# Block maxima and row sums of an attention kernel: partition reductions on GpSimd for f32 transpositions and products on TensorE

## The chip, the cores and the metric

The kernel runs on one core of one Trainium2 chip. A core has five engines with a queue of instructions each, which run in order within an engine and meet one another only through semaphores: TensorE (PE in the profile, its weight loads PEld), VectorE (DVE), ScalarE (ACT), GpSimd (POOL) and SyncE (SP), which here issues the DMAs. The metric is the time of one execution on the device in microseconds (us), the median of several runs.

## What is computed

One graph attention layer behind a layer norm, with 4096 rows of 512 numbers in float32 and a dense 4096x4096 mask:

```python
h = relu(layernorm(x))                        # 4096 x 512
q = h @ W_q.T + b_q;  k = h @ W_k.T + b_k;  v = h @ W_v.T + b_v
z = (q @ k.T) / sqrt(512) * adj               # 4096 x 4096
z = where(z == 0, -10000, z)
out = x + relu(softmax(z, axis=1) @ v)
```

The softmax of a row needs two numbers from all of its 4096 scores: their largest, and the sum of the exponentials.

## The kernel before

**Layout.** The 4096 queries are worked on in BLOCKS = 8 blocks `s` of QW = 512. Within a block the 4096 keys are taken in PAIRS = 16 pairs `j` of tiles with 128 keys each. Step `n = 16 s + j` is one pair of one block, 128 steps in all. Scores are held transposed: keys on the 128 partitions, the block's 512 queries along the row. A pair is a slot of 128 x 1024 f32 (two tiles), and `slots` is a ring of 20. So everything that a query needs from all keys has to be reduced in two stages: over pairs by DVE (`run_min`, `acc`), and over the 128 partitions.

**A step in the steady stretch.** PE forms the scores of pair `i = n + 19` in four pieces (`scores`, L503: seven products of 6 matmuls in f16 halves, as the score product is done with seven quarter products in place of eight), and between them adds step n's probabilities times v into four PSUM banks (`weigh_v`, L559, four calls of 6 matmuls, one for each 128 queries `t`). ACT copies each product out of PSUM (`copy_m1` L747, `copy_m2` L752, `copy_u2` L759, `copy_m7` L764, `copy_u4` L769, `copy_d` L774, `copy_c12` L781), forms the exponentials of step n+2 (`exp` L786) and their f16 upper half (`high_p` L793). DVE adds the products (`add_c11` L1085, `add_c2` L1093), multiplies by the mask (`weigh` L1101), turns zeros into the large value and flips the sign (`negate` L1105), keeps the running smallest (`see_min` L1114, L1117; in flipped sign the largest score is the smallest number), subtracts the floor (`lower` L1133), forms the lower f16 half (`low_p` L1140) and adds up the exponentials (`add_up` L1148, L1151).

**The end of a block's scores.** When j = 14 the scores of block s+1 are complete. DVE folds the two halves of `run_min` into `half_min` (`halve_min`, L1121, 128 x 512). PE transposes it in four pieces of 128 x 128 into a PSUM bank (`turn_min`, L571), DVE takes the smallest along each row (`columns_min`, L1126, into `col_min`), PE transposes each column, repeated 128 times, back (`widen_min`, L579), and ACT copies the bank to `floor_b` (`copy_floor`, L799). Each partition then holds the smallest value of each query, and `lower(16 (s+1))` can start. Behind it on ACT stand `exp` and `high_p` of the same pair, then `copy_c12` and the next pair's `copy_m1`.

**The row sums.** In the same step DVE folds `acc` into `row_acc` (`halve_acc`, L1157). In step j = 15 PE multiplies it, four pieces of 128 x 128, with a column of ones (`sum_rows`, L587), DVE takes the reciprocal out of PSUM (`row_gain`, L1163, L1165, into `row_out`), and ACT scales the four banks with it (`copy_o`, L808). `weigh_v` of the next block's first pair waits for `copy_o`, bank by bank.

**Order.** The order of each engine's instructions is written out by hand in the loops over n. The first block is different only in that its scores are formed while the projections still run; from step n = 109 on no scores are left, and PE runs `weigh_v` alone. GpSimd has almost nothing to do: memsets, the identity matrix `ident`, and two `partition_all_reduce` of 128 x 4 and 128 x 5 numbers for the scales of v and of the key-query product (L449). That operation leaves in every partition the reduction over all partitions, column by column.

Of the kernel before, what the change touches and what calls it, by code (L numbers as in the profile page):

```python
# [11 lines left out]
ABSMAX = bass.bass_isa.ReduceOp.absmax  # L12

P = 128
# [34 lines left out]
def adj_preln_attention(nc, x, adj_t, wq, bq, wk, bk, wv_t, bv, out, g_dram, v_dram, h_dram):  # L49
# [15 lines left out]
    with ctx:  # L65
# [6 lines left out]
        def sem(name):  # L72
            return ctx.enter_context(nc.semaphore(name))
# [20 lines left out]
        ones = sb("ones", [P, 1], F32)  # L94
        log_p = sb("log_p", [P, 1], F32)
        col_min = sb("col_min", [P, QT], F32)
# [80 lines left out]
        ones_ready = sem("ones_ready")  # L177
# [57 lines left out]
        min_turned = sem("min_turned")  # L235
        col_min_ready = sem("col_min_ready")
        min_wide = sem("min_wide")
# [7 lines left out]
        sums_ready = sem("sums_ready")  # L245
        inv_ready = sem("inv_ready")
# [191 lines left out]
        def _(pool):  # L438
            nc.gpsimd.memset(zeros[:, :], 0.0).then_inc(zeros_ready, 1)
            nc.gpsimd.memset(ident[:, :], 0.0).then_inc(ident_zero, 1)  # L440
            nc.gpsimd.memset(ones[:, :], 1.0).then_inc(ones_ready, 1)
            nc.gpsimd.memset(log_p[:, :], LOG_P_SCALE).then_inc(ones_ready, 1)
# [3 lines left out]
                                    ).then_inc(ident_ready, 1)  # L446
            for k in range(2):
                pool.wait_ge(mag_ready, k + 1)
                nc.gpsimd.partition_all_reduce(mag_all[k][:, :], mag[k][:, :], P, ABSMAX).then_inc(mag_reduced, 1)  # L449

        @block.tensor
        def _(pe):
# [55 lines left out]
            def scores(i, piece):  # L508
# [3 lines left out]
                if piece == 0:  # L512
# [10 lines left out]
                    if s >= 2 and j == 2:  # L523
                        pe.wait_ge(floor_ready, s)
                    if s >= 2 and j == 3:
                        pe.wait_ge(inv_ready, s - 1)
# [36 lines left out]

            def turn_min(s, bank):
                pe.wait_ge(half_min_ready, s + 1)
                if s == 0:
                    pe.wait_ge(v_lo_ready, TILES)
                else:
                    pe.wait_ge(c12_copied, min(PAIRS * s + PAIRS + 1, STEPS))
                for b in range(QT):  # L570
                    mm = pe.transpose(bank[:, b * P:(b + 1) * P], half_min[:, b * P:(b + 1) * P], ident[:, :])  # L571
                mm.then_inc(min_turned, 1)

            def widen_min(s, bank):
                pe.wait_ge(col_min_ready, s + 1)
                if s == 0:
                    pe.wait_ge(g_copied, KC * QUADS)
                for b in range(QT):
                    mm = pe.transpose(bank[:, b * P:(b + 1) * P], col_min[:, b:b + 1].to_broadcast([P, P]),  # L579
                                      ident[:, :])  # L580
                mm.then_inc(min_wide, 1)

            def sum_rows(s):
                pe.wait_ge(row_acc_ready, s + 1)
                pe.wait_ge(c12_copied, min(PAIRS * s + 2 * PAIRS + 2, STEPS))
                for b in range(QT):
                    mm = pe.matmul(a_bank[1][:, b:b + 1], row_acc[:, b * P:(b + 1) * P], ones[:, :],  # L587
                                   start=True, stop=True)
                mm.then_inc(sums_ready, 1)
# [58 lines left out]
            turn_min(0, o_bank[2])  # L648
            scores(PAIRS + 2, 0)
            scores(PAIRS + 2, 1)  # L650
            widen_min(0, o_bank[3])
            scores(PAIRS + 2, 2)
            scores(PAIRS + 2, 3)
            for n in range(STEPS):
# [12 lines left out]
                if j == PAIRS - 2 and s + 1 < BLOCKS:  # L667
                    widen_min(s + 1, a_bank[0])
# [8 lines left out]
        def _(act):  # L677
# [117 lines left out]
            def copy_floor(s, bank):  # L795
                act.wait_ge(min_wide, s + 1)
                if s > 0:
                    act.wait_ge(lowered, PAIRS * s)
                nc.scalar.copy(floor_b[:, :], bank[:, :]).then_inc(floor_ready, 1)  # L799

# [76 lines left out]
            for n in range(-3, STEPS):  # L877
# [16 lines left out]
                if first:  # L894
                    copy_floor(s + 1, a_bank[0])
                if n == -1:
                    copy_floor(0, o_bank[3])
# [28 lines left out]
        def _(dve):  # L926
# [196 lines left out]

            def columns_min(s, bank):
                dve.wait_ge(min_turned, s + 1)
                v.tensor_reduce(col_min[:, :], bank[:, :].rearrange("p (b n) -> p b n", b=QT), AX_X, ALU.min  # L1126
                                ).then_inc(col_min_ready, 1)
# [185 lines left out]
            columns_min(0, o_bank[2])  # L1313
# [8 lines left out]
            for n in range(STEPS):  # L1322
# [14 lines left out]
                if first:  # L1337
                    columns_min(s + 1, a_bank[0])
# [63 lines left out]
```

## Time and profile before

| | |
|---|---|
| Median of 3 runs | 1510.57 us (1510.37 to 1510.74) |
| The profiled execution | 1511.22 us, of which the span of the trace is 1509.4 us |
| PE, DVE, ACT, POOL busy | 98%, 84%, 58%, 0% of the span |
| Chain that ended last | PE 92% |
| Mean granted TensorE clock | 0.994 of full speed |

The span is the time from the first to the last instruction. The chain that ended last is followed back from the last instruction, at each step to what released it. A row of the timeline gives the start, the duration (overlapping the next instruction's start by 0.1 to 0.2 us on PE and DVE), engine, line, operation and tiles, and in brackets how long the engine had stood idle before and for whom.

### The profile page before, as it was taken

The page shows a single profiled execution, that of the slowest core. Times are in us where ns is not written, and L with a number is a line of the kernel's source. Part 1 is how long each engine was busy: PE and PEld are TensorE (multiplying, and loading weights), DVE is VectorE, ACT ScalarE, POOL GpSimd, SP SyncE. Part 2 cuts the span into 40 slices and gives each one's busy share as a digit, 9 for nine tenths or more (in the row PEclk, how much of TensorE's full clock was granted, in tenths as well). Part 3 has the DMA queues.
Part 4 walks back from the last instruction along what each step waited for, and adds up shares of the span by engine and source line. Part 5 has one row for each costly group of instructions (what it writes and reads, how often), then busy time and mean ns, then how long its engine had stood idle before and what let it go on. Part 6 is the DMA issues. An engine that isn't in the chain of part 4 may idle for free.

```text
span 1509.4 us, 24873 instructions
## 1 busy us (share of the span) xinstructions
PE 1481.5 (98%) x9550; PEld 943.5 (63%) x9550; DVE 1273.4 (84%) x1570; ACT 879.8 (58%) x1402; POOL 1.7 (0%) x11
## 2 busy tenths in 40 slices
PE   8899999889999999999999999999999999999998
PEld 4456665556666666666666666666666666666544
DVE  5978886888897889888988898889978897988875
ACT  2566665665566556565656555655665566555542
POOL 0000000000000000000000000000000000000000
PEclk9999999999999999999999999999999999999999
DMA  5255544475554656556656665566556655664252
GB/s 202 99 207 204 181 155 164 167 283 210 217 216 182 249 213 226 210 222 227 219 201 237 237 226 196 211 237 238 209 210 221 229 210 209 215 220 185 86 168 84
DMA packets 75526, 304.92 MB, mean 202 GB/s; under 512 B 8464, under 2 KB 8464, under 8 KB 73616
## 3 DMA queue, kind: packets, MB, share of 16 engines
q1 hardware_dynamic: 75408, 303.33, 54.8%
q8 instruction: 76, 1.25, 0.3%
q14 instruction: 42, 0.34, 0.1%
HBM read 264.51 MB, written 38.80 MB: 201 GB/s over the span
## 4 chain that ended last, share of the span: by engine, by line
PE 92%; DVE 3%; issue 2%; DMA 1%; ACT 1%; SPq 0%; POOLq 0%; DVEq 0%; POOL 0%; ACTq 0%
PE o L559 44%; PE za L503 22%; PE zd L503 11%; PE zb L503 5%; PE o L490 4%; PE o L476 4%; PE o L458 1%; DVE stats L954 0%; DMA o_rows<-in_x 0%; DMA g_buf<-g_dram 0%; DMA g_dram<-spare 0%; PE za L587 0%; ACT g_buf L724 0%; DVE h_buf L1003 0%; DVE half_min L990 0%
## 5 line engine op out<-in xcount | busy, mean ns | idle before, releaser
L559 PE MATMUL o<-v_buf,p_buf 128*128 128x512 f16 x3072 | 736.5, 380 | 3.3 <-issue 3.3
L559 PEld LDWEIGHTS o<-v_buf,p_buf 128*128 128x128 f16 x3072 | 300.9, 98 | 273.0 <-issue 5.2
L503 PE MATMUL za<-h_buf,g_buf 128*128 128x256 f16 x2976 | 407.6, 273 | 7.5 <-DVE g_buf L1029 3.4
L503 PEld LDWEIGHTS za<-h_buf,g_buf 128*128 128x128 f16 x2976 | 290.4, 98 | 145.7 <-DVE g_buf L1029 5.1
L503 PE MATMUL zd<-h_buf,g_buf 128*128 128x256 f16 x1488 | 203.6, 273 | 0.0
L1093 DVE TENSOR_TENSOR slots<-um_tmp,dm_tmp 128x512 f32<-128x512 f32 x128 | 88.4, 691 | 111.7 <-ACT dm_tmp L774 111.6
L1140 DVE TENSOR_TENSOR p_buf<-slots,p_buf 128x1024 f16<-128x1024 f32 x128 | 156.1, 1220 | 21.7 <-PE o L559 20.1
L786 ACT ACTIVATE slots<-slots,log_p 128x1024 f32<-128x1024 f32 x128 | 145.9, 1140 | 37.3 <-DVE slots L1133 37.3
L781 ACT ACTIVATE slots<-za,c_all,kappa 128x256 f32<-128x256 f32 x128 | 72.4, 565 | 145.5 <-PE za L503 144.7
L503 PEld LDWEIGHTS zd<-h_buf,g_buf 128*128 128x128 f16 x1488 | 146.0, 98 | 17.2
L1105 DVE SCALAR_TENSOR_TENSOR slots<-slots 128x1024 f32<-128x1024 f32 x128 | 156.0, 1219 | 0.2
L1133 DVE TENSOR_TENSOR slots<-slots,floor_b 128x1024 f32<-128x1024 f32 x128 | 155.9, 1218 | 0.4 <-ACT floor_b L799 0.4
L747 ACT ACTIVATE mm_tmp<-za,c_all,kappa 128x256 f32<-128x256 f32 x128 | 72.5, 566 | 140.5 <-PE za L503 137.7
L1151 DVE TENSOR_TENSOR acc<-acc,slots 128x1024 f32<-128x1024 f32 x112 | 136.6, 1219 | 0.5
L1117 DVE TENSOR_TENSOR run_min<-run_min,slots 128x1024 f32<-128x1024 f32 x112 | 136.5, 1219 | 0.0
L793 ACT CAST p_buf<-slots 128x1024 f16<-128x1024 f32 x128 | 132.9, 1038 | 3.7 <-PE o L559 3.2
L1101 DVE TENSOR_TENSOR slots<-slots,adj_own 128x1024 f32<-128x1024 f32 x91 | 111.4, 1224 | 15.1 <-ACT slots L781 7.8
L759 ACT ACTIVATE um_tmp<-za,c_all,kappa 128x256 f32<-128x256 f32 x128 | 72.4, 566 | 70.6 <-PE za L503 64.1
L503 PE MATMUL zb<-h_buf,g_buf 128*128 128x256 f16 x744 | 102.2, 274 | 0.0
L769 ACT ACTIVATE um_tmp<-za,c_all,kappa 128x256 f32<-128x256 f32 x128 | 72.4, 566 | 48.5 <-PE za L503 47.7
L503 PEld LDWEIGHTS zb<-h_buf,g_buf 128*128 128x128 f16 x744 | 73.0, 98 | 8.8
L476 PE MATMUL o<-slots,h_buf 128*128 128x512 f16 x288 | 66.1, 379 | 2.0 <-DVE v_buf L1009 2.0
(151 smaller groups left out, 1107.4 us busy)
## 6 DMA issues: line engine op xcount, KB each, us to landing
g_buf<-g_dram SPq DMA_DIRECT2D x112, 896.0 KB, 5.4
v_buf<-v_dram SPq DMA_DIRECT2D x128, 512.0 KB, 3.4
adj_own<-in_adj SPq DMA_DIRECT2D x91, 512.0 KB, 6.2
spare<-in_adj SPq DMA_DIRECT2D x37, 512.0 KB, 6.3
g_dram<-g_buf SPq DMA_DIRECT2D x12, 896.0 KB, 4.7
v_dram<-v_buf SPq DMA_DIRECT2D x16, 512.0 KB, 5.2
spare<-in_x SPq DMA_DIRECT2D x15, 512.0 KB, 8.8
h_buf<-h_dram SPq DMA_DIRECT2D x7, 1024.0 KB, 8.8
```

The source lines that it names most:

```text
L476: mm = pe.matmul(v_bank(t)[:, :], h[:, a, k, span], wv_pair[:, b, k, :], start=(k == 0 and m == 0), stop=(k == KC - 1 and m == 2))
L503: mm = pe.matmul(bank[:, 0:QH], g_of(i)[:, a, op, j, :], right[b][j], start=(fresh and j == 0 and m == 0), stop=(j == 1 and m == 2), skip_ ...
L559: mm = pe.matmul(o_bank[t][:, :], a[:, kt, span], v_buf[:, n % V_BUFS, kt, b, :], start=(j == 0 and kt == 0 and m == 0), stop=(j == PAIRS ...
L786: nc.scalar.activation(slot(n), slot(n), ACT.Exp, bias=log_p[:, 0:1], scale=-UNIT).then_inc(p_ready, 1)
L793: nc.scalar.copy(p_hi[n % 3], slot(n)).then_inc(p_hi_ready, 1)
L1093: v.tensor_tensor(slot(i)[:, 1, :], um_tmp[:, :, :].rearrange("p a n -> p (a n)"), dm_tmp[:, :, :].rearrange("p a n -> p (a n)"), ALU.add) ...
L1101: v.tensor_tensor(slot(i), slot(i), adj_buf[adj_slot(i)], ALU.mult).then_inc(weighted, 1)
L1105: v.scalar_tensor_tensor(out=slot(i), in0=slot(i), scalar=0.0, in1=slot(i), op0=ALU.is_equal, op1=ALU.subtract).then_inc(negated, 1)
L1117: v.tensor_tensor(run_min[:, :, :], run_min[:, :, :], slot(i), ALU.min).then_inc(min_seen, 1)
L1133: v.tensor_tensor(slot(n), slot(n), floor_b[:, :].unsqueeze(1).to_broadcast([P, 2, QW]), ALU.subtract).then_inc(lowered, 1)
L1140: v.tensor_tensor(p_lo[n % 2], slot(n), p_hi[n % 3], ALU.subtract).then_inc(p_lo_ready, 1)
L1151: v.tensor_tensor(acc[:, :, :], acc[:, :, :], slot(n), ALU.add).then_inc(summed, 1)
```

## The change

The reduction over partitions goes to GpSimd, both for the largest scores and for the row sums. `turn_min`, `widen_min` and `sum_rows` leave PE, `columns_min` leaves DVE, `copy_floor` leaves ACT.

- After `halve_min` DVE multiplies `half_min` by -1 (a new pass over 128 x 512), as the reduction offered is a maximum. GpSimd's `find_floor(s)` reduces `half_min` into `floor_b`, and `lower` adds where it subtracted.
- GpSimd's `sum_rows(s)` reduces `row_acc` with a sum into `half_min`, which is free by then: it waits until the floor of block s+1 is there. Each partition then holds all 512 sums. `row_gain` keeps on each partition its own query's four (a product with `ident`, 128 x 512) and sums along the row (`row_sum`, a reduction over 128 x 512); the reciprocal and the scaling are as before.
- GpSimd's own order is floor 0, floor 1, sums 0, floor 2, sums 1, and so on: 16 reductions of 128 x 512.

```diff
+            def find_floor(s):
+                pool.wait_ge(half_max_ready, s + 1)
+                if s > 0:
+                    pool.wait_ge(lowered, PAIRS * s)
+                nc.gpsimd.partition_all_reduce(floor_b[:, :], half_min[:, :], P, LARGEST).then_inc(floor_ready, 1)
+            def sum_rows(s):
+                pool.wait_ge(row_acc_ready, s + 1)
+                pool.wait_ge(floor_ready, min(s + 2, BLOCKS))
+                nc.gpsimd.partition_all_reduce(half_min[:, :], row_acc[:, :], P, TOTAL).then_inc(sums_ready, 1)
...
@@ tensor
                 if more:
                     scores(n + LEAD, 0)
-                if j == PAIRS - 1:
-                    sum_rows(s)
                 weigh_v(n, 0)
-                if j == PAIRS - 2 and s + 1 < BLOCKS:
-                    turn_min(s + 1, a_bank[0])
                 if more:
                     scores(n + LEAD, 1)
                 weigh_v(n, 1)
-                if j == PAIRS - 2 and s + 1 < BLOCKS:
-                    widen_min(s + 1, a_bank[0])
...
@@ scalar
-                if first:
-                    copy_floor(s + 1, a_bank[0])
...
@@ vector, halve_min, lower, row_gain
                 v.tensor_tensor(half_min[:, :], run_min[:, 0, :], run_min[:, 1, :], ALU.min
                                 ).then_inc(half_min_ready, 1)
+                dve.wait_ge(half_min_ready, s + 1)
+                v.tensor_scalar(half_min[:, :], half_min[:, :], -1.0, None, ALU.mult).then_inc(half_max_ready, 1)
...
-                v.tensor_tensor(slot(n), slot(n), floor_b[:, :].unsqueeze(1).to_broadcast([P, 2, QW]), ALU.subtract
+                v.tensor_tensor(slot(n), slot(n), floor_b[:, :].unsqueeze(1).to_broadcast([P, 2, QW]), ALU.add
                                 ).then_inc(lowered, 1)
...
+                sums = half_min[:, :].rearrange("p (t q) -> p t q", t=QT)
                 dve.wait_ge(sums_ready, s + 1)
+                v.tensor_tensor(sums, sums, ident[:, :].unsqueeze(1).to_broadcast([P, QT, P]), ALU.mult
+                                ).then_inc(own_sums_ready, 1)
+                dve.wait_ge(own_sums_ready, s + 1)
+                v.tensor_reduce(row_sum[:, :], sums, AX_X, ALU.add).then_inc(row_sum_ready, 1)
+                dve.wait_ge(row_sum_ready, s + 1)
...
-                v.reciprocal(row_inv[:, :], a_bank[1][:, 0:QT]).then_inc(inv_ready, 1)
+                v.reciprocal(row_inv[:, :], row_sum[:, :]).then_inc(inv_ready, 1)
```

PE's queue where block 1's floor is found (steps 14 and 15), before: `za` and `zb`, `zd` are the banks of the scores, `o` those of the output.

```order
L559 MATMUL o0<-v_buf,p_buf 128x512 x6
L571 MATMUL za0<-ident,half_min 128x128 x4
L503 MATMUL za1<-h_buf0,g_buf 128x256 x6
L503 MATMUL zd<-h_buf0,g_buf 128x256 x6
L559 MATMUL o1<-v_buf,p_buf 128x512 x6
L579 MATMUL za0<-ident,col_min 128x128 x4
L503 MATMUL za1<-h_buf0,g_buf 128x256 x6
...
L503 MATMUL zb<-h_buf0,g_buf 128x256 x6
L587 MATMUL za1<-ones,row_acc 128x1 x4
L559 MATMUL o0<-v_buf,p_buf 128x512 x6
```

The same place after:

```order
L572 MATMUL o0<-v_buf,p_buf 128x512 x6
L520 MATMUL za1<-h_buf0,g_buf 128x256 x6
L520 MATMUL zd<-h_buf0,g_buf 128x256 x6
L572 MATMUL o1<-v_buf,p_buf 128x512 x6
L520 MATMUL za1<-h_buf0,g_buf 128x256 x6
```

Twelve f32 matrix operations are gone from between the products of a block; nothing else moved on PE.

DVE's queue in the same two steps, before, with the semaphores that each instruction waits for:

```order
L1121 TENSOR_TENSOR half_min<-run_min 128x512 [waits min_seen]
L1101 TENSOR_TENSOR slots<-slots,adj_own 128x1024 [waits c2_added,adj_loaded1,c11_added,c12_copied]
L1140 TENSOR_TENSOR p_buf<-slots,p_buf 128x1024 [waits o_done,p_hi_ready]
L1126 TENSOR_REDUCE col_min<-za 128x4 [waits min_turned]
...
L1157 TENSOR_TENSOR row_acc<-acc 128x512 [waits summed]
L1085 TENSOR_TENSOR slots<-mm_tmp 128x256 [waits summed,m2_copied,m1_copied]
L1133 TENSOR_TENSOR slots<-slots,floor_b 128x1024 [waits min_seen,floor_ready,negated]
...
L1163 RECIPROCAL row_inv<-za 128x4 [waits sums_ready]
```

The same place after:

```order
L1089 TENSOR_TENSOR half_min<-run_min 128x512 [waits min_seen]
L1092 TENSOR_SCALAR half_min<-half_min 128x512 [waits half_min_ready]
L1069 TENSOR_TENSOR slots<-slots,adj_own 128x1024 [waits c2_added,adj_loaded1,c11_added,c12_copied]
L1105 TENSOR_TENSOR p_buf<-slots,p_buf 128x1024 [waits o_done,p_hi_ready]
...
L1122 TENSOR_TENSOR row_acc<-acc 128x512 [waits summed]
L1053 TENSOR_TENSOR slots<-mm_tmp 128x256 [waits summed,m2_copied,m1_copied]
L1098 TENSOR_TENSOR slots<-slots,floor_b 128x1024 [waits min_seen,floor_ready,negated]
...
L1128 TENSOR_TENSOR half_min<-half_min,ident 128x512 [waits sums_ready]
L1131 TENSOR_REDUCE row_sum<-half_min 128x4 [waits own_sums_ready]
L1135 RECIPROCAL row_inv<-row_sum 128x4 [waits row_sum_ready]
```

The pass over PSUM (`col_min`) is replaced by the change of sign, which stands earlier and waits for no other engine; the two waits for GpSimd are at the first `lower` (`floor_ready`) and at the first instruction of `row_gain` (`sums_ready`).

## Rows read from the trace of the kernel before

**Rows 1.** The page, part 1: busy us, share of the span, instructions.

```profile
PE 1481.5 (98%) x9550; PEld 943.5 (63%) x9550; DVE 1273.4 (84%) x1570; ACT 879.8 (58%) x1402; POOL 1.7 (0%) x11
```

**Rows 2.** Timeline of PE at the end of block 1's scores (start, duration).

```profile
468.23 0.60 PE L571 MATMUL za<-ident,half_min 128*128 128x128 f32 x4
468.66 0.82 PE L503 MATMUL za<-h_buf,g_buf 128*128 128x256 f16 x6
...
471.27 0.60 PE L579 MATMUL za<-ident,col_min 128*128 128x128 f32 x4
471.70 0.82 PE L503 MATMUL za<-h_buf,g_buf 128*128 128x256 f16 x6
...
477.57 0.95 PE L587 MATMUL za<-ones,row_acc 128*128 128x1 f32 x8
478.38 1.45 PE L559 MATMUL o<-v_buf,p_buf 128*128 128x512 f16 x6
479.67 0.82 PE L503 MATMUL za<-h_buf,g_buf 128*128 128x256 f16 x6
```

**Rows 3.** Timeline of DVE in the same stretch, with idle time before.

```profile
463.79 0.68 DVE L1121 TENSOR_TENSOR half_min<-run_min 128x512 f32<-128x512 f32 x1
...
468.86 0.69 DVE L1126 TENSOR_REDUCE col_min<-za 128x4 f32<-128x512 f32 x1 [1.38 <-PE za L571]
...
472.80 1.22 DVE L1133 TENSOR_TENSOR slots<-slots,floor_b 128x1024 f32<-128x1024 f32 x1
```

**Rows 4.** Timeline of ACT in the same stretch.

```profile
474.05 1.15 ACT L786 ACTIVATE slots<-slots,log_p 128x1024 f32<-128x1024 f32 x1 [0.36 <-DVE slots L1133]
...
477.12 0.57 ACT L747 ACTIVATE mm_tmp<-za,c_all,kappa 128x256 f32<-128x256 f32 x1 [0.37 <-PE za L503]
```

**Rows 5.** Groups of instructions on POOL: busy us, mean ns of one, idle before.

```profile
L449 POOL PARTITION_ALL_REDUCE mag_all_v<-mag_v x1 | 0.4, 403 | 12.5 <-DVE mag_v L936 12.5
L449 POOL PARTITION_ALL_REDUCE mag_all_m<-mag_m x1 | 0.4, 386 | 17.2 <-DVE mag_m L936 17.2
...
L439 POOL MEMSET zeros<- 128x128 f32 x1 | 0.2, 205 | 0.3 <-POOLq L1389 0.3
...
L441 POOL MEMSET ones<- 128x1 f32 x1 | 0.1, 99 | 0.0
```

**Rows 6.** Timeline of DVE, then of POOL, around the first small reduction.

```profile
22.89 0.67 DVE L990 SCALAR_TENSOR_TENSOR half_min<-acc,floor_b 128x512 f32<-128x512 f32 x1
...
22.36 0.40 POOL L449 PARTITION_ALL_REDUCE mag_all_v<-mag_v  x1 [12.54 <-DVE mag_v L936]
```

**Rows 7.** Timelines of DVE and PE at the end of the last block's scores.

```profile
1408.70 0.69 DVE L1121 TENSOR_TENSOR half_min<-run_min 128x512 f32<-128x512 f32 x1
...
1415.43 8.79 PE L559 MATMUL o<-v_buf,p_buf 128*128 128x512 f16 x40
```

**Rows 8.** Timeline of DVE at the opening of the steady stretch.

```profile
312.20 0.69 DVE L1121 TENSOR_TENSOR half_min<-run_min 128x512 f32<-128x512 f32 x1
...
321.23 1.23 DVE L1133 TENSOR_TENSOR slots<-slots,floor_b 128x1024 f32<-128x1024 f32 x1 [0.40 <-ACT floor_b L799]
```

**Rows 9.** Timelines of DVE and ACT at the end of the program.

```profile
1495.92 0.69 DVE L1157 TENSOR_TENSOR row_acc<-acc 128x512 f32<-128x512 f32 x1
...
1500.61 0.69 ACT L808 ACTIVATE o_rows<-o,row_out 128x512 f32<-128x512 f32 x1 [11.36 <-PE o L559]
```

**Rows 10.** Timeline of PE after its two longest waits late in the opening.

```profile
292.17 1.35 PE L503 MATMUL za<-h_buf,g_buf 128*128 128x256 f16 x6 [3.40 <-DVE g_buf L1029]
...
327.29 2.72 PE L559 MATMUL o<-v_buf,p_buf 128*128 128x512 f16 x6 [3.27 <-issue]
```

**Rows 11.** Stretches of PE: start and end, us, PE busy, granted clock, DMA share, GB/s.

```profile
324.00:327.00 3.00, 0.03 (x1) 0.91 0.85 328
327.00:330.00 3.00, 2.71 (x7) 0.50 1.04 436
330.00:333.00 3.00, 3.00 (x15) 0.50 0.16 60
```

More of the change, by code:

```diff
@@ L12 @@
 ABSMAX = bass.bass_isa.ReduceOp.absmax
+LARGEST = bass.bass_isa.ReduceOp.max
+TOTAL = bass.bass_isa.ReduceOp.add
 P = 128
@@ L93, in adj_preln_attention @@
         zeros = sb("zeros", [P, P], F32)
-        ones = sb("ones", [P, 1], F32)
         log_p = sb("log_p", [P, 1], F32)
-        col_min = sb("col_min", [P, QT], F32)
+        row_sum = sb("row_sum", [P, QT], F32)
         row_inv = sb("row_inv", [P, QT], F32)
@@ L176, in adj_preln_attention @@
         zeros_ready = sem("zeros_ready")
-        ones_ready = sem("ones_ready")
+        log_ready = sem("log_ready")
         wide_ready = sem("wide_ready")
@@ L234, in adj_preln_attention @@
         half_min_ready = sem("half_min_ready")
-        min_turned = sem("min_turned")
-        col_min_ready = sem("col_min_ready")
-        min_wide = sem("min_wide")
+        half_max_ready = sem("half_max_ready")
         floor_ready = sem("floor_ready")
@@ L245, in adj_preln_attention @@
         sums_ready = sem("sums_ready")
+        own_sums_ready = sem("own_sums_ready")
+        row_sum_ready = sem("row_sum_ready")
         inv_ready = sem("inv_ready")
@@ L440, in _ @@
             nc.gpsimd.memset(ident[:, :], 0.0).then_inc(ident_zero, 1)
-            nc.gpsimd.memset(ones[:, :], 1.0).then_inc(ones_ready, 1)
-            nc.gpsimd.memset(log_p[:, :], LOG_P_SCALE).then_inc(ones_ready, 1)
+            nc.gpsimd.memset(log_p[:, :], LOG_P_SCALE).then_inc(log_ready, 1)
             pool.wait_ge(ident_zero, 1)
@@ L449, in _ @@
                 nc.gpsimd.partition_all_reduce(mag_all[k][:, :], mag[k][:, :], P, ABSMAX).then_inc(mag_reduced, 1)
+            find_floor(0)
+            for s in range(BLOCKS):
+                if s + 1 < BLOCKS:
+                    find_floor(s + 1)
+                sum_rows(s)
         @block.tensor
@@ L522, in scores @@
                         pe.wait_ge(c12_copied, i - 1)
[L523 to L526, printed above, removed]
                     product(i, a, A11, of_h(s, 0, 0), True).then_inc(za_ready, 1)
@@ L562, in weigh_v @@
                 mm.then_inc(o_done, 1)
[L564 to L589, printed above, removed]
             def product_m(d):
@@ L647, in _ @@
                     scores(i, piece)
-            turn_min(0, o_bank[2])
             scores(PAIRS + 2, 0)
             scores(PAIRS + 2, 1)
-            widen_min(0, o_bank[3])
             scores(PAIRS + 2, 2)
@@ L793, in high_p @@
                 nc.scalar.copy(p_hi[n % 3], slot(n)).then_inc(p_hi_ready, 1)
[L795 to L799, printed above, removed]
             def copy_o(s, t):
@@ L1122, in halve_min @@
                                 ).then_inc(half_min_ready, 1)
[L1124 to L1127, printed above, removed]
+                dve.wait_ge(half_min_ready, s + 1)
+                v.tensor_scalar(half_min[:, :], half_min[:, :], -1.0, None, ALU.mult).then_inc(half_max_ready, 1)
             def lower(n):
@@ L1312, in _ @@
             add_c2(PAIRS + 1)
-            columns_min(0, o_bank[2])
             weigh(PAIRS + 1)
@@ L1336, in _ @@
                     row_gain(s)
-                if first:
-                    columns_min(s + 1, a_bank[0])
                 if scored:
```

2 lines of the change are left out of this document (removed).

## The prediction

> **What bounds the kernel now.** I read the busy times first: PE 98% of the span, DVE 84%, ACT 58%, POOL nothing [rows 1]. Then the timeline of PE where a block's scores end: each instruction starts as the one before it leaves, with no bracket of idle time [rows 2]. So in the steady stretch PE's own work is the time, and an f32 operation taken from it shortens the run, as long as nothing that PE waits for comes later. Then the timelines of DVE and ACT at the same place, for how much later it may come [rows 3, 4], and the opening, the last block and the tail, where the slack differs [rows 7 to 9]. Last POOL, for what a reduction costs [rows 5].
>
> **What leaves PE.** Start to start, `turn_min` holds PE 468.66 - 468.23 = 0.43 us, `widen_min` 471.70 - 471.27 = 0.43 us, `sum_rows` 478.38 - 477.57 = 0.81 us [rows 2]. That is 1.67 us a block, 13.4 us for eight: the most that the change can give. ACT loses a copy and DVE `columns_min` (0.61 start to start) with the 1.38 us it waited for PE [rows 3]; neither bounds. DVE gains the change of sign and, in `row_gain`, two passes over 128x512. Nearest row for each is a pass of that size, 0.68 us, 0.61 start to start [rows 3].
>
> **What one wide reduction costs (X).** The trace has this operation only at 128x4 and 128x5: 0.403 and 0.386 us [rows 5]. From below: filling 128 columns takes 0.205 us and one column 0.099, so 0.83 ns a column; 512 columns make 0.4 + 0.4 = 0.8 us. From above: if all of the 0.386 us grew with its 5 columns, 512 would take 39.5 us. The two rows differ by 17 ns, and in the wrong direction, so a column costs hardly more than half of that scatter, some 7 to 8 ns: 512 columns would be 3.6 to 4.1 us. I take X = 4 us, call it an estimate, and keep 0.8 and 39.5; I give 1 in 12 to X under 1.9, 6 in 10 to X under 5.8, 1 in 6 to X over 10.
>
> [...]
>
> **How late a floor may come.** On DVE `halve_min` starts at 463.79; with the change of sign behind it POOL can start near 465.2 [rows 3]. DVE asks for the floor at `lower(16)`, 472.80 before, about 470.8 after, as `columns_min` and its wait are gone. Behind `lower` stand the exponential, its cast, `copy_c12` and `copy_m1(34)` on ACT: from the end of `lower` at 474.02 to 477.69 are 3.67 us, of which 0.37 idle, so 3.3 [rows 3, 4]. PE wants that copy at 479.67 - 1.67 = 478.0 [rows 2]. So `lower` may end at 474.7, and X may be about 8 us there. Queued behind a waiting `lower` on DVE are `add_c2(33)`, `lower(17)` and `weigh(33)`, all needed later than this. The row sums start on POOL when both `row_acc` and the floor are there, and end before PE needs `copy_o` near 486.4 as long as X is under 8.5; above that each us of X counts twice, floor and sums, as one follows the other on POOL.
>
> The other places have less room. Opening: `half_min` at 312.20, the floor asked for near 320.4 (DVE idled 0.40 for it before) [rows 8]: free up to X = 7, worth 0.8 us. Last block's floor: steps there last 5.2 us, since PE has no scores left. `half_min` is at 1408.70, floor at 1410.0 + X, sums at 1410.0 + 2X, then `row_gain` 1.6 and `copy_o` 0.7: 1412.3 + 2X. PE wants it for step 112, which stood four calls of 1.295 us after 1415.43, at 1420.6, less 1.67 [rows 7]: 1418.9. PE stalls 2X - 6.6, at X = 4 about 1.5 us, and the gain of this block is gone. Tail: `row_acc` is ready at 1496.6, `row_out` then at 1496.7 + X + 1.6; before, the first `copy_o` started at 1500.61 [rows 9], and DVE's additions and the stores follow it in a chain. The end moves by X - 2.3: +1.7 us at X = 4.
>
> **Sum if DVE is not disturbed,** X = 4: six block ends -10.0, opening -0.8, last block's floor 0, tail +1.7: -9.1, that is 1501.5. It breaks even near X = 6.6.
>
> **What else the reductions may do.** DVE and POOL read and write the same SBUF, and behind the change of sign all that stands in DVE's queue up to the second `lower` reads two tiles from SBUF. If such a pass cannot run while a reduction reads its tile, DVE loses X to the floor and X to the sums, both in front of `lower`. The rows are silent on it: the one reduction that ran with DVE at work, 22.36 to 22.76, lay beside a copy out of PSUM, and the next pass with two tiles started at 22.89, after it [rows 6]. So I take it as even, with slightly more on the blocking side. Price: `lower(16)` would end at 472.0 + 2X and may end at 474.7, a stall of 2X - 2.6, less 1.67: +3.7 us a block end at X = 4, six times, 22.4. Opening X - 0.9 = +3.1. Last block: the passes between the two reductions (`low_p`, `add_up`, `halve_acc`, 3.0 us) no longer lie beside the first, so 2X - 6.6 + 3.0, and the second holds up two `lower` (2.3) and `low_p` ahead of `row_gain` (1.1), together 2X - 0.2 less 1.67: +6 to +7. Tail +1.7. Sum +33.5; breakeven near X = 1.9, each further us 16.
>
> [...] After a wait of 3.40 us a group of 6 took 1.35 where 0.82 is usual: at least 0.5 lost. At X = 4 PE would wait 5.4 us in each block, longer than either, so I take a value nearer to the upper end, 2.3, for seven waits: +16. So 1510.6 + 33.5 + 16 = **1560 us**. The sums are made against the profiled execution (1511.2 us, span 1509.4); the median is 0.6 below it, and I add to the median.
>
> [...]
>
> **The rivals.**
> A: undisturbed DVE and X under 5.8. For it: POOL is idle, the small reductions return in 0.4 us, DVE's slack before `lower` is large. Time 1501.5, at X = 2 about 1499.
> B: undisturbed DVE, but X over 7.3. The wait for the floor, then for the sums, takes the place of the f32 operations: at X = 9 about +15 (the last block and the tail give +18, the steady blocks then gain 0.8 each in place of 1.67), at X = 12 about +60 = 1570.
> C: DVE is held up, X over 2: the forecast; X = 3 gives 1535, X = 8 about 1625, X = 10 about 1656.
> D: held up, but X under 1.9: faster by a few us.
> That the change doesn't do what it says: the queues show that PE's twelve operations a block are gone, so I give this nothing.
>
> **How the numbers follow.** C 0.49, B 0.13, A 0.29, D 0.03, and 0.06 for a result within 0.2% (3 us, about what a measurement can tell from no change), which X between 5.8 and 7.3 undisturbed or near 1.9 held up would give. Faster 0.32, same 0.06, slower 0.62. The range for 8 in 10: the low end is A with X of 2 to 3, the high end C at X = 10; beyond lie the longer reductions, up to 39.5 us. So 1500 to 1660.
>
> **What the profile after would show.** The duration and spacing of the 16 wide reductions on POOL: X at 4. If C holds, passes of DVE with two SBUF tiles beside a reduction start late or last X longer, while the change of sign and the copies of ACT don't; PE idles some 5 us before the products of step 15, waiting for ACT's `copy_m1`, and the clock falls behind it. If A holds, the 128x1024 passes keep 1.22 us, PE has no idle time between 340 and 1400, and a block takes 156.3 us where it took 157.9. If B holds, DVE idles at `lower` for POOL. Wrong would be the forecast if X were under 2, or if DVE ran undisturbed.

## The result and the profile after

The change makes the kernel faster: 1502.21 us, median of 6 runs (1501.08 to 1503.62), against 1510.65 for the kernel before in 6 runs beside them (1509.15 to 1512.25). The ratio is 0.9944, interval 0.9934 to 0.9954: a gain of 0.6%, small but clear of the scatter. The forecast of 1560 us, slower, was wrong; the range from 1500 to 1660 just holds the time, by rival A at its low end. The profiled execution took 1502.08 us with a span of 1500.3, 9.1 us less than the span before; the medians differ by 8.4.

The page of the kernel after, parts 1 and 4 (busy us, share of the span, instructions; then the shares of the chain that ended last), beside [rows 1]:

```profile
PE 1467.7 (98%) x9422; PEld 928.3 (62%) x9422; DVE 1301.7 (87%) x1586; ACT 871.3 (58%) x1394; POOL 45.1 (3%) x26
...
PE 86%; issue 6%; DVE 4%; DMA 1%; ACT 1%; POOL 0%; POOLq 0%; SPq 0%; DVEq 0%; ACTq 0%
```

PE's busy time fell by 13.8 us and is still 98% of the span: PE still sets the pace. DVE's rose by 28.3 us. The timeline of POOL shows how long a reduction is (start, duration; seven of the sixteen):

```profile
313.47 2.71 POOL L452 PARTITION_ALL_REDUCE floor_b<-half_min  x1 [272.82 <-DVE half_min L1092]
463.11 1.79 POOL L452 PARTITION_ALL_REDUCE floor_b<-half_min  x1 [146.92 <-DVE half_min L1092]
469.45 3.34 POOL L457 PARTITION_ALL_REDUCE half_min<-row_acc  x1 [4.56 <-DVE row_acc L1122]
619.40 1.78 POOL L452 PARTITION_ALL_REDUCE floor_b<-half_min  x1 [146.62 <-DVE half_min L1092]
...
1398.28 2.68 POOL L452 PARTITION_ALL_REDUCE floor_b<-half_min  x1 [144.00 <-DVE half_min L1092]
1402.12 4.13 POOL L457 PARTITION_ALL_REDUCE half_min<-row_acc  x1 [1.16 <-DVE row_acc L1122]
1486.28 3.23 POOL L457 PARTITION_ALL_REDUCE half_min<-row_acc  x1 [80.03 <-DVE row_acc L1122]
```

A maximum takes 1.79 us, a sum 3.34, not 4 and 4; the longer ones, 2.71, 2.68 and 4.13, are taken up at e1. A block takes 619.40 - 463.11 = 156.3 us where it took 157.9. And DVE is held up beside them. Its timeline at the end of block 1's scores, which answers to [rows 3]:

```profile
461.87 0.68 DVE L1089 TENSOR_TENSOR half_min<-run_min 128x512 f32<-128x512 f32 x1
...
463.20 2.02 DVE L1069 TENSOR_TENSOR slots<-slots,adj_own 128x1024 f32<-128x1024 f32 x1 [0.19 <-ACT slots L759]
465.15 1.21 DVE L1105 TENSOR_TENSOR p_buf<-slots,p_buf 128x1024 f16<-128x1024 f32 x1
...
469.61 3.26 DVE L1098 TENSOR_TENSOR slots<-slots,floor_b 128x1024 f32<-128x1024 f32 x1
```

Two passes are long and no others: `weigh` beside the maximum takes 2.02 us where 1.22 is usual (+0.80), `lower(16)` beside the sum 3.26 (+2.04). The pass at 465.15 is already at its usual 1.21; beside the sum no other pass than `lower(16)` is touched. So per block DVE loses 2.84 us, although POOL is busy for 1.79 + 3.34 = 5.13. Does PE lose anything by it? The timelines of ACT and then of PE, for [rows 4] and [rows 2]:

```profile
472.91 1.15 ACT L764 ACTIVATE slots<-slots,log_p 128x1024 f32<-128x1024 f32 x1 [2.02 <-DVE slots L1098]
...
475.51 0.55 ACT L725 ACTIVATE mm_tmp<-za,c_all,kappa 128x256 f32<-128x256 f32 x1
```

```profile
474.77 1.46 PE L572 MATMUL o<-v_buf,p_buf 128*128 128x512 f16 x6
476.12 0.83 PE L520 MATMUL za<-h_buf,g_buf 128*128 128x256 f16 x6
```

ACT idles 2.02 us for the late `lower`, and its `copy_m1` ends at 476.06. PE starts on it at 476.12, 1.35 after the call before, where 1.30 is a call's spacing. The whole slack is used up, and PE loses 0.05 us.

**Where the 9.1 us come from**, each from the same operation in both traces:

| Stretch | before | after | difference |
|---|---|---|---|
| start to `half_min` of block 1 | 463.79 | 461.87 | -1.9 |
| `half_min` of block 1 to that of block 7 (six blocks) | 944.91 | 935.16 | -9.8 |
| from there to the last `row_acc` | 87.22 | 88.47 | +1.3 |
| from there to the end | 13.5 | 14.8 | +1.3 |

Six blocks give 1.63 each, the 1.67 of [rows 2] less PE's wait of 0.05. In the last block DVE is held in the same way, and the floor and the sums come just behind each other. DVE's timeline of after, which answers to [rows 7]:

```profile
1397.03 0.69 DVE L1089 TENSOR_TENSOR half_min<-run_min 128x512 f32<-128x512 f32 x1
...
1399.36 1.94 DVE L1116 TENSOR_TENSOR acc<-acc,slots 128x1024 f32<-128x1024 f32 x1
...
1401.94 4.40 DVE L1098 TENSOR_TENSOR slots<-slots,floor_b 128x1024 f32<-128x1024 f32 x2
...
1409.05 0.23 DVE L1137 TENSOR_SCALAR row_out<-row_inv,up_inv 128x4 f32<-128x4 f32 x1
```

Two `lower` take 4.40, start to end, instead of 2.35 (e5, where no sum runs beside them). `row_out` comes at 1409.3, the copies of the block's output (`copy_o`) behind it, and PE waits for them, in its timeline:

```profile
1410.19 10.09 PE L572 MATMUL o<-v_buf,p_buf 128*128 128x512 f16 x46 [2.76 <-ACT o_rows L780]
```

In the tail DVE stands idle for POOL, 3.36 us; the `row_gain` behind it is two passes longer than before, and ACT's copies come last, in DVE's and ACT's timelines, for [rows 9]:

```profile
1485.50 0.69 DVE L1122 TENSOR_TENSOR row_acc<-acc 128x512 f32<-128x512 f32 x1
1489.55 0.69 DVE L1128 TENSOR_TENSOR half_min<-half_min,ident 128x512 f32<-128x512 f32 x1 [3.36 <-POOL half_min L457]
...
1491.52 2.44 ACT L780 ACTIVATE o_rows<-o,row_out 128x512 f32<-128x512 f32 x4 [12.69 <-DVE row_out L1137]
```

Of the 1.9 at the start 0.86 are the two transpositions of block 0 that are gone. The rest goes with the stretch at half speed late in the opening (granted clock 0.50), which was shorter. Stretches of PE of the kernel after, which answer to [rows 11] (columns as there):

```profile
327.00:330.00 3.00, 3.00 (x11) 0.50 0.93 373
330.00:333.00 3.00, 3.00 (x22) 0.95 0.16 63
```

Block 0's `half_min` stands at 312.20 before and at 312.23 after, so all of the 1.9 arises behind it: from there to that of block 1 are 151.59 us before and 149.64 after. In the experiments with the whole change (e1, e2, e6, e7, e8) this stretch takes 148.9 to 149.6. (e6 has its block 1 at 462.78, 0.9 later than the kernel after, but it is late by that much at block 0 already: the time to there differs from run to run.) The kernel before has one trace only, so whether its longer stretch at half speed, and with it the other 1.1 us, belongs to it or is chance isn't shown.

### The profile page after: what moved, and what is told of

It reads as the page before. It is cut to its first block, busy times and chain, and to the rows that moved or that the text cites. A ratio compares the mean times of both kernels' runs of the same rounds, so it can differ in the third digit from the quotient of the medians.

```text
span 1500.3 us, 24631 instructions
## 1 busy us (share of the span) xinstructions
PE 1467.7 (98%) x9422; PEld 928.3 (62%) x9422; DVE 1301.7 (87%) x1586; ACT 871.3 (58%) x1394; POOL 45.1 (3%) x26
## 4 chain that ended last, share of the span: by engine, by line
PE 86%; issue 6%; DVE 4%; DMA 1%; ACT 1%; POOL 0%; POOLq 0%; SPq 0%; DVEq 0%; ACTq 0%
PE o L572 38%; PE za L520 22%; PE zd L520 11%; PE zb L520 5%; PE o L507 4%; PE o L493 4%; PE o L475 1%; DVE stats L922 1%; DMA o_rows<-in_x 0%; DMA g_buf<-g_dram 0%; DMA g_dram<-spare 0%; PE zd L599 0%; POOL half_min L457 0%; ACT g_buf L702 0%; PE za L579 0%
## 5 line engine op out<-in xcount | busy, mean ns | idle before, releaser
L1098 DVE TENSOR_TENSOR slots<-slots,floor_b 128x1024 f32<-128x1024 f32 x128 | 170.2, 1330 | 0.0
L1069 DVE TENSOR_TENSOR slots<-slots,adj_own 128x1024 f32<-128x1024 f32 x91 | 114.5, 1259 | 12.5 <-ACT slots L759 4.8
```

The lines of the kernel that those rows point to most:

```text
L1069: v.tensor_tensor(slot(i), slot(i), adj_buf[adj_slot(i)], ALU.mult).then_inc(weighted, 1)
```

## The experiments

The edits are shown against the changed kernel, with names and indices shortened.

**The theory (R):** a wide reduction holds up DVE's passes over two SBUF tiles for a part of its time only, about 0.85 us of a maximum and 2.05 of a sum (+0.80 and +2.04 in the trace above); if a DVE pass has begun first, it is the reduction that takes longer. That this part is the reading of the tile is the author's assumption; no trace shows it. **The rivals:** DVE is shut out for the whole reduction (the forecast, with a smaller X); or what counts is all that POOL does in a block, wherever it lies.

**e1: the disputed costs by themselves.** A prelude ahead of the kernel runs reductions alone, and then single ones beside one kind of pass on DVE.

```
+ for op, n in ((LARGEST, 512), (LARGEST, 256), (LARGEST, 128), (TOTAL, 512), (TOTAL, 256), ...):
+     pool.wait_ge(probe_go, turn[0])
+     partition_all_reduce(dst[:, 0:n], src[:, 0:n], P, op)
...
+ two = v.tensor_tensor(slots[:, 12 + u], pb_, pc, ALU.add)        # 128x1024, two tiles of SBUF
+ one = v.tensor_scalar(slots[:, 12 + u], pb_, 2.0, None, ALU.mult)
+ red = v.tensor_reduce(dots[:, 2 * u:2 * u + 2], pb_, AX_X, ALU.add)
+ mix = v.tensor_tensor(..., d_bank[:, :], pb_[:, 0, :], ALU.add)   # one operand in PSUM
+ short = v.tensor_tensor(..., pb_[:, 0, :], pc[:, 1, :], ALU.add)  # 128x512
```

> The changed kernel with a prelude before everything else: GpSimd makes single reductions, first with VectorE idle (maximum over 512, 256, 128 columns, sum over 512, 256, 128, maximum and sum over 512 again), then a sum beside four two-tile passes of 128x1024, a maximum and a sum beside eight two-tile passes of 128x512, a sum beside four one-tile passes, beside four reductions along the row, beside six passes with one operand from PSUM. Theory R (exclusive while reading): alone a maximum takes 1.75 us and a sum 3.2; of the short two-tile passes exactly one is longer, by 0.85 beside a maximum and 2.05 beside a sum, and all others keep 0.69; the forms with one SBUF tile keep their times. Rival S (the engines share the bandwidth): two or more short passes are longer, none by the whole amount, until the reduction ends, and the reduction is longer than alone. Rival W (the forecast: held for the whole reduction): one pass is longer by the whole 1.8 or 3.3. Durations go with the columns: a sum over 128 some 1.1 us.

Measured, POOL's timeline of this kernel; the first three stand alone (maxima over 512 and 128 columns, a sum over 512), the fourth is beside two-tile passes already running, the last beside passes with one operand in PSUM:

```profile
17.91 1.80 POOL L471 PARTITION_ALL_REDUCE slots<-slots  x1 [8.25 <-issue]
...
21.21 0.70 POOL L471 PARTITION_ALL_REDUCE slots<-slots  x1 [0.22 <-DVE newton L1192]
22.13 3.24 POOL L471 PARTITION_ALL_REDUCE slots<-slots  x1 [0.22 <-DVE newton L1192]
...
34.34 4.14 POOL L471 PARTITION_ALL_REDUCE slots<-slots  x1 [0.22 <-DVE newton L1192]
...
63.70 3.23 POOL L471 PARTITION_ALL_REDUCE slots<-slots  x1 [1.41 <-DVE newton L1192]
```

From 1.80 at 512 and 0.70 at 128 columns a maximum costs 2.9 ns a column over a base of 0.33 us; the sum, 3.24 and 1.07 at the same sizes, 5.7 ns a column. On DVE, the passes by kind (number: shortest, median and longest ns, start of the first and the last; forms):

```profile
L1200 DVE TENSOR_TENSOR slots<-slots x4: 1209/1216/3262, 34.2 to 39.6; 128x1024 f32<-128x1024 f32 x4
...
L1205 DVE TENSOR_TENSOR slots<-slots x16: 678/679/2730, 40.9 to 53.0; 128x512 f32<-128x512 f32 x16
...
L1201 DVE TENSOR_SCALAR slots<-slots x4: 673/992/2732, 53.7 to 58.2; 128x1024 f32<-128x1024 f32 x4
...
L1202 DVE TENSOR_REDUCE dots<-slots x4: 1210/1212/1216, 58.9 to 62.3; 128x2 f32<-128x1024 f32 x4
...
L1203 DVE TENSOR_TENSOR slots<-zd,slots x6: 681/681/686, 63.5 to 66.5; 128x512 f32<-128x512 f32 x6
```

Beside a sum one pass of four, or of eight, is longer, by 3262 - 1216 = 2.05 us or 2730 - 679 = 2.05, at 1024 columns as at 512; all others keep their time. That speaks against rival S of the expectation, by which two or more short passes would have been longer. The held one is this,

```profile
47.31 2.73 DVE L1205 TENSOR_TENSOR slots<-slots 128x512 f32<-128x512 f32 x1
```

and the next, from 49.97 on, takes its usual 0.68 although POOL's sum (46.86 to 50.49) is still running. Beside the maximum the short passes lost 0.85 once. That the part that holds DVE is the reading of the tile stays a name for it: no row shows what POOL does inside a reduction, and tiles of one size hold for 2.05 in a sum and 0.85 in a maximum. In its turn the sum took 4.14 for 3.24, 0.90 longer: it started at 34.34, while a pass was running that ended at 35.38 (34.16 + 1.22). Beside a sum, row reductions kept their 1.21 us and passes with an operand in PSUM their 0.68. One expectation failed: the `tensor_scalar`, one tile in and one out, is held too, one pass by 2.05 and the next by about 0.6, until about when the sum ends. Why is open. The kernel has one such pass at this place, the change of sign, and it runs ahead of the reduction.

**e2: the floor found twice.** It puts one more maximum, 1.9 us of POOL, ahead of `lower`.

```
 def find_floor(s):
+    partition_all_reduce(floor_b, half_min, P, LARGEST).then_inc(again, 1)
+    pool.wait_ge(again, s + 1)
     partition_all_reduce(floor_b, half_min, P, LARGEST).then_inc(floor_ready, 1)
```

> The changed kernel with each of the eight floor reductions made twice, one after the other, into the same tile; nothing is left out. Theory R (a wide reduction keeps VectorE's two-tile passes waiting only while it reads, 0.85 us for a maximum and 2.05 us for a sum): VectorE loses another 0.85 us in front of the first lowering of each block, which in the changed kernel already ends with 0.05 us of slack for TensorE, so a block takes 157.1 us in place of 156.3 and the run 6 to 8 us more than the changed kernel, about 1509. Rival D (the reductions disturb nobody, only their duration counts): the floor is there at 466.7 where it is asked for at 469.6, so blocks stay at 156.3 us and the run within 2 us of the changed kernel.

Measured: 1510.99 us in 11 runs against 1510.24 before, ratio 1.0003 (0.9994 to 1.0012). All of the change's gain is gone. Timelines of POOL, DVE and PE of this kernel at block 1's scores:

```profile
463.22 1.78 POOL L453 PARTITION_ALL_REDUCE floor_b<-half_min  x1 [144.48 <-DVE half_min L1095]
465.09 1.89 POOL L455 PARTITION_ALL_REDUCE floor_b<-half_min  x1
...
620.35 1.78 POOL L453 PARTITION_ALL_REDUCE floor_b<-half_min  x1 [146.60 <-DVE half_min L1095]
```

```profile
463.32 2.02 DVE L1072 TENSOR_TENSOR slots<-slots,adj_own 128x1024 f32<-128x1024 f32 x1 [0.19 <-ACT slots L762]
465.26 2.06 DVE L1108 TENSOR_TENSOR p_buf<-slots,p_buf 128x1024 f16<-128x1024 f32 x1
```

Each maximum lengthens one pass by 0.80 to 0.85, no more. The block takes 620.35 - 463.22 = 157.13 us, 0.83 more than after: with the slack used up, the 0.84 us by which DVE is held once more go into PE's time. The rival of full holding would have had 1.8 here. PE's timeline has the wait that was not there in the kernel after:

```profile
477.06 0.83 PE L523 MATMUL za<-h_buf,g_buf 128*128 128x256 f16 x6 [0.72 <-ACT mm_tmp L728]
```

The total came 2 us above what was expected of it. That lies in the last block, from `half_min` to the last `row_acc` 92.43 us where after has 88.47: PE waits 1.04 us longer, and the clock falls behind the wait, which costs about 2.9, the rest. PE's timeline and one of its stretches (columns as in [rows 11]):

```profile
1416.34 24.02 PE L575 MATMUL o<-v_buf,p_buf 128*128 128x512 f16 x97 [3.80 <-ACT o_rows L783]
...
1416.00:1420.00 4.00, 3.66 (x9) 0.50 0.00 0
```

**e6: the sums made twice.** Is it that every microsecond on POOL costs, or only that which lies ahead of `lower(16)`?

```
 def sum_rows(s):
+    partition_all_reduce(half_min, row_acc, P, TOTAL).then_inc(again, 1)
+    pool.wait_ge(again, s + 1)
     partition_all_reduce(half_min, row_acc, P, TOTAL).then_inc(sums_ready, 1)
```

> The changed kernel with each row sum reduction made twice, one after the other; nothing is left out. If what counts is what stands ahead of the block's first lowering: the second reduction reads after that lowering (472.9 to 475.0 in the changed kernel's times), holds only passes that have some us to spare, and the sums, 3.3 us later, are still there before the row gain needs them to be. Steady blocks stay at 156.3 us; the last block's floor and the tail lose 3.3 us each: 6.6 us over the changed kernel, about 1508.8. If every us that VectorE is held counts, a block takes 158.3 us and the run is another 12 us longer, about 1521.

Measured: 1511.40 us in 11 runs against 1510.04, ratio 1.0011 (1.0002 to 1.0020). The blocks are as expected: POOL's `find_floor` stands at 464.02 and 620.32, 156.30 apart, as after, although DVE is held 2.05 us longer. DVE's timeline shows whom the second sum holds:

```profile
470.52 3.27 DVE L1101 TENSOR_TENSOR slots<-slots,floor_b 128x1024 f32<-128x1024 f32 x1
...
474.32 3.26 DVE L1101 TENSOR_TENSOR slots<-slots,floor_b 128x1024 f32<-128x1024 f32 x1
```

`lower(17)`, which nothing waits for yet. The total was 2.6 above the expectation. In the profiled execution 0.9 of it stands ahead of block 0's `half_min`, and 1.3 in the last block beyond the longer wait: PE waits there for the block's output copies, in its timeline, and the stretches (columns: us, then busy us and instructions of PE, of its weight load, DVE, ACT and POOL; granted clock; DMA) have the clock behind it:

```profile
1414.33 2.29 PE L575 MATMUL o<-v_buf,p_buf 128*128 128x512 f16 x5 [5.97 <-ACT o_rows L783]
...
1412.00:1416.00 4.00, 1.67 (x5) 0.60 (x6) 3.86 (x7) 2.50 (x5) 0.00 (x0) 0.71 0.00 0
1416.00:1420.00 4.00, 4.00 (x18) 1.73 (x17) 2.07 (x2) 3.15 (x3) 0.00 (x0) 0.87 0.00 0
```

A wait of 5.97 us, then stretches with a mean clock of 0.71 and 0.87. They mix two levels: in finer stretches it is 0.50 from 1414 to 1416 and 1.00 from 1418 on. After the 2.76 us of the kernel after no drop is seen; its stretch from 1412 to 1416 has 1.00.

**e7: as e2, with the sums begun behind `lower(16)`.** If DVE's being held by the sum ahead of `lower(16)` is what uses up the slack, this must give the steady blocks back their 156.3 us, the doubled floor notwithstanding.

```
 def find_floor(s):
+    partition_all_reduce(floor_b, half_min, P, LARGEST).then_inc(again, 1)
+    pool.wait_ge(again, s + 1)
     ...
 def sum_rows(s):
     pool.wait_ge(floor_ready, min(s + 2, BLOCKS))
+    if s + 1 < BLOCKS:
+        pool.wait_ge(lowered, PAIRS * (s + 1) + 1)
```

> The kernel with the floor reductions made twice (1511.0 us, blocks of 157.1 us), and the row sum reduction of a block held back until the next block's first lowering is done; one more wait on GpSimd, nothing is left out. Theory R: the 2.05 us of the sum's reading no longer stand ahead of that lowering, so it ends 1.2 us earlier than in the changed kernel even with two floor reductions, and blocks are back at 156.3 us; at the last block the sums come about 1 us later than there. Run 1503 to 1505.5. If the price of the doubled floor lies in its duration on GpSimd and not in VectorE being held, blocks stay at 157.1 and the run at 1511 or above.

Measured: 1506.59 us in 8 runs (1503.19 to 1508.64), ratio 0.9974 (0.9964 to 0.9984). The timeline of POOL, then of DVE:

```profile
463.51 1.78 POOL L453 PARTITION_ALL_REDUCE floor_b<-half_min  x1 [144.63 <-DVE half_min L1097]
...
472.27 3.51 POOL L462 PARTITION_ALL_REDUCE half_min<-row_acc  x1 [5.00 <-DVE slots L1103]
...
619.75 1.78 POOL L453 PARTITION_ALL_REDUCE floor_b<-half_min  x1 [143.98 <-DVE half_min L1097]
```

```profile
470.86 1.22 DVE L1103 TENSOR_TENSOR slots<-slots,floor_b 128x1024 f32<-128x1024 f32 x1
...
472.60 3.26 DVE L1103 TENSOR_TENSOR slots<-slots,floor_b 128x1024 f32<-128x1024 f32 x1
```

619.75 - 463.51 = 156.24: 0.9 less than e2, with one wait more. POOL does as much work as in e2, and the price of 0.83 a block is gone: PE paid there for what was held ahead of `lower(16)`, not for POOL's time. The median is 1.1 above the expected range. The total scatters more than usual: three executions took 1503.2 to 1505.0 us at a mean clock of 0.994 to 0.995, five 1505.6 to 1508.6 at 0.991 to 0.992. The profiled one is of the first three; its PE waits 3.84 us at the last block's floor and the clock stays at 1.00 behind it. That it falls there in the other five I take from their means, and from e2, where it fell behind a wait of 3.80; no trace of e7 shows it.

**e3: the reductions over 4 columns.** What would the kernel take if they cost nearly nothing?

```
- partition_all_reduce(floor_b[:, :], half_min[:, :], P, LARGEST)
+ partition_all_reduce(floor_b[:, 0:4], half_min[:, 0:4], P, LARGEST)
- partition_all_reduce(half_min[:, :], row_acc[:, :], P, TOTAL)
+ partition_all_reduce(half_min[:, 0:4], row_acc[:, 0:4], P, TOTAL)
...
- activation(slot(n), slot(n), ACT.Exp, bias=log_p, scale=-UNIT)
+ activation(slot(n), slot(n), ACT.Exp, bias=log_p, scale=0.0)
```

> The changed kernel with all sixteen wide reductions over 4 columns in place of 512. It leaves out the reduction of the other 508 columns, and the exponential is taken with scale 0 so that it stays finite; every other instruction is as in the changed kernel. It shows what the change would bring if a reduction cost 0.4 us. Theory R: steady blocks stay at 156.3 us, as TensorE has no idle time there; the last block's floor and the tail give back 1.4 and 1.2 us or more, since nothing is waited for: 1498 to 1500 us. Rival D says the same for the blocks, and the same for the tail; a block under 156.2 us would say that the wide reductions cost TensorE something even in the steady stretch.

Measured: 1498.41 us in 5 runs, ratio 0.9923 (0.9909 to 0.9936), as expected; the block takes 156.24, only 0.06 less than with full reductions. So the whole width costs the steady blocks nothing that matters, and what is left to gain lies at the ends of the program.

**e4: floors on POOL, sums back on PE.** One part of the change alone.

```
+ def on_pool(s):
+     return False
...
+ if j == PAIRS - 1 and not on_pool(s):
+     sum_rows(s)                       # PE's products with ones, as before
```

> Half of the change: floors by GpSimd, row sums by TensorE as before, so the passes over 128x512 in the row gain are gone too. Theory R: a block gains only the two f32 transposition groups, 0.86 of 1.67 us, so 157.1 us; opening -1.9, six blocks -5.2, last block's floor -0.9, tail 0: about 8 us under before, 1502.5 to 1503.5, as fast as the whole change. A rival says that the sum reductions bring more than they cost (steady 0.81 us a block, six times 4.9, less 2.6 at the end): then this kernel is 2 us slower than the changed one. The two differ by the end of the program alone; the blocks tell it: 157.1 us.

Measured: 1503.80 us in 5 runs, ratio 0.9957 (0.9944 to 0.9969), 0.3 above the expected range. Floors on POOL stand 1092.62 - 935.57 = 157.05 us apart: 0.88 less than before, the two transpositions of 0.43. The sums are worth the other 0.8 a block, though they hold DVE until its slack is gone. Over six blocks that is 4.6 us, less the 2.6 that the ends of the program give back: so the whole change should be 2.0 faster than this half, which is the rival's sum, and 1.6 was measured. The intervals of the two ratios overlap, so the totals alone don't decide it.

**e5: the sums of the last two blocks on PE.** The same switch as in e4, with another condition; it should take back what the last block and the tail gave away.

```
-     return False
+     return s < BLOCKS - 2
```

> The changed kernel with the row sums of the last two blocks made by TensorE as before, those of the first six by GpSimd. If the part of the gain that was given back lies at the last block's floor (TensorE idle 2.8 us for the output copies behind the row gain) and in the tail (VectorE idle 3.4 us for the last sum reduction), this kernel keeps the 11.7 us that the changed one is ahead when the last block's scores end, adds 0.9 for the last floor and loses nothing after it: 12 to 12.5 us under before, 1498 to 1498.7. If the loss there has another cause (the floor reduction itself), it stays near 1501.

Measured: 1498.99 us in 5 runs, ratio 0.9929 (0.9916 to 0.9941), 0.3 above the expected range. In PE's timeline the wait of 2.76 us is gone, for 0.90 us of products:

```profile
1402.02 1.04 PE L592 MATMUL za<-ones,row_acc 128*128 128x1 f32 x8
1402.92 22.28 PE L583 MATMUL o<-v_buf,p_buf 128*128 128x512 f16 x102
```

**e8, e10, e9: after, only the last sums on PE, and e5, on one chip.** They split the two ends from each other.

> The changed kernel again, unchanged, so that the two mixed kernels stand beside it on one chip: 1502.2, ratio to before 0.9944.

> The changed kernel with only the last block's row sums made by TensorE. It tells the two places apart at which gain was given back. The tail alone is put right: from the start of the last row_acc to the end 13.5 us as before, in place of 14.8, less 0; so 1.2 us under the changed kernel, 1501.0. TensorE still waits 2.8 us for the output copies at the last block's floor.

> Row sums of the last two blocks by TensorE, as in the run before it, beside the changed kernel on one chip: 3.2 us under it, 1499.0, of which 1.2 in the tail and 2.0 at the last block's floor (2.8 us of waiting gone, 0.8 of products back).

Against 1509.45 before: e8 1502.62 (ratio 0.9955, 0.9941 to 0.9969), e10 1501.23 (0.9943, 0.9930 to 0.9956), e9 1498.78 (0.9927, 0.9914 to 0.9940). The tail is worth 1.4 us and the last block's floor 2.5 by the medians, where 1.2 and 2.0 were expected. The intervals of e8 and e10 overlap, those of e8 and e9 just part. e9 is the best version: 10.7 us under before and 3.8 under the change.

e8 is the same kernel as after, and its trace shows something that after's doesn't: the clock falls behind the same wait. PE's timeline and a stretch of it (columns as in [rows 11]):

```profile
1410.22 20.10 PE L572 MATMUL o<-v_buf,p_buf 128*128 128x512 f16 x86 [2.77 <-ACT o_rows L780]
...
1408.00:1412.00 4.00, 1.78 (x5) 0.70 0.40 131
```

From the last block's `half_min` to the last `row_acc` are 89.84 us there, against 88.47 after: 1.4 us for the clock. e10, with the same wait, has 89.90 and a clock of 0.76 in that stretch. So the +1.3 of the table above is +2.6 in such an execution, and the sums of block 6 on PE take away the wait and this risk with it.

## Why the prediction was wrong

The forecast had the sign wrong mainly by one term: a stall of 2X - 2.6 = 5.4 us at each of six block ends, and the clock behind it. PE waits 0.05 us there. Two steps made the term too large, the length of a reduction and how much of it holds DVE.

**What leaves PE: right.** 1.67 us a block was removed and 1.63 came back, six times. PE was the bound, as read from [rows 1, 2].

**X = 4 for both reductions: wrong, the first failed step.** The argument took half the scatter between two small reductions [rows 5] as a price per column of 7 to 8 ns. It is 2.9 for a maximum and 5.7 for a sum; X is 1.8 and 3.3. Two rows that differ by one column, with the larger one faster, carry no slope. That both operations cost the same was assumed as well, without a word.

**DVE held for the whole reduction: right that it is held, wrong for how long, the second failed step.** "DVE loses X to the floor and X to the sums" priced 2X. Measured: 0.80 and 2.04 us, 2.84 for 5.13 of reductions. That DVE is held at all no row of before showed; the forecast took it as even. The traces bear it out for passes with two SBUF tiles, and where such a pass had begun first it was the reduction that took longer (the sum with 4.14 for 3.24); they don't bear out the whole length, for beside a maximum of 1.80 us a pass was longer by 0.85 only.

**The sum of C, with the right sizes, comes out close.** It breaks even at X = 1.9 and charges 16 us for each us of X. With X of (1.8 + 3.3) / 2 = 2.55 it would give 1510.6 + 10.3 = 1521; with half of the 2.84 us that DVE is really held, 1.42, it gives 1510.6 - 7.8 = 1502.8, and 1502.2 was measured. That it comes so near is in part luck. By term the sum then has -8.6 for the six block ends, +0.5 for the opening, +1.0 for the last block and -0.9 for the tail; measured were -9.8, -1.9, +1.3 and +1.3. The opening and the tail are each off by over 2 us, and cancel. The stall formula itself stands (2X - 2.6 with 2.84 for 2X gives 0.2 us a block, measured 0.05), and the slack behind `lower` was read right: `lower` was to end by 474.7, 10.9 us after `half_min` starts, and it ends 11.0 after it. e2, held 0.85 more, gives 0.83 us more a block. To correct one step alone would not have saved the sign: the sizes alone give the 1521, and X at 4 with DVE held for 2.84 / 5.13 of it still 1510.6 + 33.5 - 16 x 1.8 = 1515.

**The clock, +16: wrong with the rest.** It hung on PE waiting 5.4 us in every block; PE waits 0.05. No run shows the 2.3 us for one wait; the author put it between the 0.5 that a group lost after 3.40 us [rows 10] and 3.0, half of the six at a granted clock of 0.50 [rows 11]. It was of the right size: where PE waited for the output copies at the last block and the clock fell, it cost 1.4 us (e8, e10), 1.3 (e6) and 2.9 (e2). In the traces of after, e1 and e7 it didn't fall behind waits of 2.8 to 3.8 us, and cost nothing. That the price was "nearer to the upper end" was a choice with nothing behind it.

**The last block and the tail: nearly right.** Stall 2X - 6.6 gives nothing at the measured 5.1 for 2X, and +6 to +7 in all was forecast for C; PE waited 2.76 us, and against before the block gives back 1.3 us. C's own formula, 2X - 0.2, gives 2.6 with the 2.84 us that DVE is held. Both reductions ran 0.9 long, as each found a pass of DVE running (2.68 for 1.79, 4.13 for 3.24), and `low_p` stood between the sums and `row_gain`. For the tail X - 2.3 with 3.3 is +1.0, measured +1.3. The sum without disturbance breaks even near X = 7.0 by its own terms (-9.1 at X = 4, 3 us more for each us), not 6.6; nothing hung on that.

**The rivals.** A's 1501.5 lies 0.7 us off, and yet A was false: it had DVE undisturbed. It comes near because the slack swallows what it left out, and by luck at the start (1.9 us for its 0.8), which makes up for the last block (+1.3 for its 0). The case nearest to what happened was D, held up but short, which had a chance of 0.03. Its condition, "X under 1.9", was meant for the reduction's length and holds for the maximum alone; had the text said that what counts is how long DVE is held, and that this has its own lower bound, much of C would have been D.

## What to carry to other kernels

The work moved to the idle engine held up its neighbour for 2.84 us a block, not for its own length of 5.13, and PE lost 0.05 by it. So ask of such a move which passes it shuts out, for how long, and how much slack stands behind them. Two rows of almost equal size give a base and no slope; keep the chances spread over the slope's whole range. When the steady part has slack and the ends have none, switch the change off for the last block or two (3.8 us here, e9 against e8).

## What the runs showed of the hardware

- A sum across partitions cost twice a maximum per column in e1: 3.24 against 1.80 us at 128x512 f32, 5.7 against 2.9 ns a column.
- Of DVE's passes with two SBUF tiles one was longer by 0.80 to 0.85 us beside a maximum (by 0.72 at the last block of after, 1.94 for 1.22) and one by 2.05 us beside a sum; beside a sum, row reductions (1.21) and passes with a PSUM operand (0.68) were not.
- A `tensor_scalar` over 128x1024 f32 from SBUF to SBUF took 2.73 us for 0.67 beside a sum, and another pass of it was longer by about 0.6.
- A reduction that came while a pass with two SBUF tiles was running took longer: a maximum 2.71 for 1.79 at 313.47 in after, a sum 4.14 for 3.24 in e1.
- PE's granted clock was 0.50 after a wait of 3.27 us in the opening, after 3.80 at the last block of e2 and after 5.97 in e6, and fell after 2.77 in e8 and 2.76 in e10 (0.70 and 0.76 from 1408 to 1412); it stayed at 1.00 after 2.76 (after, e1) and 3.84 (e7's profiled execution). The same kernel, after and e8, shows both behind the same wait, so the length of the wait doesn't decide it; what does stays open.
